# A decoder layer whose last, quantised FFN gets its weights and input ready-made, and runs its block and token loops as one

## The reference

```python
def act_quant(x):
    scale = 127.0 / jnp.clip(jnp.max(jnp.abs(x), axis=-1, keepdims=True), 1e-05)
    return jnp.clip(jnp.round(x * scale), -128, 127) / scale
def weight_quant(w):
    scale = 1.0 / jnp.clip(jnp.mean(jnp.abs(w)), 1e-05)
    return jnp.clip(jnp.round(w * scale), -1, 1) / scale
# x = x + FFN(layernorm(x)), with w1 (2048, 512) and w2 (512, 2048)
h = bit_linear(x, w1)                    # act_quant(x) @ weight_quant(w1).T
h = depthwise_conv1d(h, conv_w, conv_b)  # 3 taps along the tokens, zeros at both ends
h = jax.nn.silu(h)
return bit_linear(h, w2)
```

## Time and profile before

| | |
|---|---|
| median of 3 runs | 3668.49 us (3667.8 to 3669.5) |
| the profiled execution | 3668.09 us, of which the span from first to last instruction is 3666.5 us |
| PE busy | 3195.8 us (87%) |
| DVE busy | 2299.4 us (63%) |
| ACT busy | 1861.1 us (51%) |
| POOL busy | 1074.4 us (29%) |
| mean granted clock of TensorE | 0.945 of full speed |
| `cross_ffn` | some 2280 to 3043 us |
| `quantised_ffn` | 3043 us to the end |

### The profile page before, as it was taken

How to read it: one execution, slowest core, us unless ns; L and a number is a source line. 1 busy time by engine, 2 the same in 40 slices (tenths; PEclk the granted TensorE clock), 3 DMA queues, 4 the chain that set the end, 5 groups by cost and what they waited for, 6 DMA issues and landing times. The chain is left out here.

```text
span 3666.5 us, 56984 instructions
## 1 busy us (share of the span) xinstructions
PE 3195.8 (87%) x19244; PEld 2328.8 (64%) x19284; DVE 2299.4 (63%) x4086; ACT 1861.1 (51%) x3035; POOL 1074.4 (29%) x831
## 2 busy tenths in 40 slices
PE   6998999999999998699978995999999992576576
PEld 5776666666666665577756774788888881244244
DVE  6444888888888886455536886323232227878876
ACT  2123888888888887122223221422222223777676
POOL 2223131131132121423213553111111111466555
PEclk9999999999999999899988998999999995798898
DMA  4544122121122121655435442211111104021111
GB/s 153 183 161 132 56 89 63 54 89 60 57 88 61 57 80 56 230 206 197 168 121 166 138 138 98 98 35 35 35 34 34 35 24 150 6 70 33 37 46 41
DMA packets 224825, 331.24 MB, mean 90 GB/s; under 512 B 26768, under 2 KB 113840, under 8 KB 224176
## 3 DMA queue, kind: packets, MB, share of 16 engines
q1 hardware_dynamic: 199536, 293.54, 24.3%
q10 hardware_dynamic: 22016, 25.17, 1.9%
q0 software_dynamic: 3136, 10.80, 0.9%
HBM read 200.20 MB, written 129.24 MB: 90 GB/s over the span
## 5 line engine op out<-in xcount | busy, mean ns | idle before, releaser
L704 DVE CUSTOM_DVE_ANT_0 attend_scores<-attend_scores,attend_bias_table 128x1024 f32<-128x1024 f32 x512 | 630.5, 1232 | 163.5 <-PE attend_scores L558 156.9
L631 ACT ACTIVATE attend_probs<-attend_scores,attend_neg_max 128x1024 f32<-128x1024 f32 x512 | 571.5, 1116 | 136.3 <-DVE attend_neg_max L704 127.0
L570 PE MATMUL attend_turned<-attend_ident,attend_probs 128*128 128x128 f32 x4096 | 557.3, 275 | 11.4 <-DVE attend_probsT L712 11.2
L570 PEld LDWEIGHTS attend_turned<-attend_ident,attend_probs 128*128 128x128 f32 x4096 | 472.6, 141 | 121.4 <-DVE attend_probsT L712 32.7
L558 PE MATMUL attend_scores<-attend_k_stack,attend_q_stack 96*128 96x512 f32 x1024 | 374.9, 448 | 14.4 <-DMA attend_q_stack<-qk_parts 9.4
L1937 DVE TENSOR_TENSOR cross_ffn_h_lo<-cross_ffn_hidden,cross_ffn_h_hi 128x512 fp32r<-128x512 f32 x128 | 91.5, 720 | 466.6 <-ACT cross_ffn_h_hi L1876 466.6
L639 ACT COPY attend_probsT<-attend_turned 128x512 f32<-128x512 f32 x640 | 359.5, 583 | 25.2 <-PE attend_turned L570 23.4
L1873 ACT ACTIVATE cross_ffn_hidden<-cross_ffn_h_acc,cross_ffn_b_cols 128x512 f32<-128x512 f32 x128 | 88.3, 690 | 484.5 <-PE cross_ffn_h_acc L1814 484.5
L585 PE MATMUL attend_out_acc<-attend_probsT,attend_v_in 128*32 128x256 f32 x4096 | 312.9, 389 | 0.7 <-DVE attend_out_full L722 0.7
L532 POOL TENSOR_TENSOR attend_out_parts<-attend_out_full,attend_out_parts 128x256 fp32r<-128x256 f32 x64 | 46.7, 729 | 855.8 <-ACT attend_out_parts L646 855.8
L712 DVE COPY attend_probsT<-attend_turned 128x512 f32<-128x512 f32 x384 | 263.4, 686 | 1.0 <-PE attend_turned L570 1.0
(11 more groups left out here) (292 smaller groups left out, 6604.1 us busy)
## 6 DMA issues: line engine op xcount, KB each, us to landing
qk_parts<-qkv_qk_out SPq DMA_DIRECT2D x64, 512.0 KB, 3.1
attend_k_stack<-qk_parts SPq DMA_DIRECT2D x192, 128.0 KB, 2.5
attend_q_stack<-qk_parts SPq DMA_DIRECT2D x192, 128.0 KB, 2.6
o_parts<-attend_out_parts ACTq DMA_DIRECT2D x64, 256.0 KB, 2.5
mix_in_o_in<-o_parts SPq DMA_DIRECT2D x32, 512.0 KB, 6.5
qkv_x_in<-x SPq DMA_DIRECT2D x8, 1024.0 KB, 5.7
v_rows<-qkv_v_out SPq DMA_DIRECT2D x32, 256.0 KB, 2.3
attend_v_in<-v_rows SPq DMA_DIRECT2D x128, 64.0 KB, 1.8
```

The costliest lines, as they stand in the source:

```text
L570: last = pe.transpose(turned[:, x, c], probs[:, i % 2, k * P:(k + 1) * P], ident[:, :])
L631: act.activation(probs[:, i % 2], scores[:, i % 2], ACT.Exp, bias=neg_max[:, i % 4:i % 4 + 1], scale=-1.0, accum_out=den[:, qg % 2, j, h:h ...
L704: dve.tensor_tensor_reduce(scores[:, i % 2], scores[:, i % 2], bias_table[:, h, at:at + T], -1.0, BIG, ALU.add, ALU.min, neg_max[:, i % 4: ...
```

## The change

Three stages are edited.

`project_qkv` also prepares the last FFN's weights. In its first batch POOL loads w1 and w2 in eight pieces of 1 MB, ACT sums their absolute values; PE adds up, DVE makes `w_mean` (`mean_weights`). In the four halves of batches 1 and 2 they are loaded again, one group of each a half, scaled (ACT), clipped and rounded (DVE, `round_group`), turned (PE, `turn_group`, at blocks 8 and 10), copied (ACT) and stored in bf16 to `w1T_parts` and `w2T_parts`. The opening is reordered: x's second half is loaded after all weights, weight chunks 1 and 3 are split on POOL, and the second half is turned inside the first products. The loop over batches is written out.

`cross_ffn` also makes the last FFN's input. Inside half n, DVE makes statistics of half n-1 of x2 (`x_factors`, at block 4) and normalises, scales and rounds it (`quantise_x`, blocks 6 to 9); PE turns it (`turn_x`, blocks 8 to 11), ACT copies, SP stores `xq_parts` and the token scales `x_units`. The ring of `h_hi` and `h_lo` goes from 4 to 2.

`quantised_ffn` loads what these made and has one loop for everything:

```diff
-            pe.wait_ge(wT_ready, GROUPS)
-            sequences(pe, body)
+        def slots(work, turn):
+            for u in range(UNITS + 1):
+                for f in range(HB):
+                    if u < UNITS:
+                        work(u, f)
+                    turn(u, f)
+            for f in range(8):
+                turn(UNITS + 1, f)
+        def tile_at(u, f, back):
+            j = (u - 1) * HT + f // 4 - back
+            return j if 0 <= j < TILES else None
 # SP, ahead of its slots
-                for k in range(4):
-                    sp.dma_start(w1_raw[:, k * 4:(k + 1) * 4], w1[k * D:(k + 1) * D, :].rearrange("(c p) n -> p c n", p=P))\
-                        .then_inc(w_loaded[k], 16)
...
+                load_x(0)
+                sp.dma_start(w1T[:, :, :], w1T_parts.rearrange("k p n -> p k n")).then_inc(w_loaded[0], 16)
+                load_x(1)
+                sp.dma_start(w2T[:, :, :], w2T_parts.rearrange("f p n -> p f n")).then_inc(w_loaded[1], 16)
 # POOL
+                def work(u, f):
+                    i = u * HB + f
+                    pool.wait_ge(right_ready, i + 1)
+                    pool.wait_ge(left_added, i + 1)
+                    pool.tensor_tensor(conv[:, i % CR], conv[:, i % CR], right_tap[:, i % 2], ALU.add).then_inc(right_added, 1)
+                def turn(u, f):
+                    j = tile_at(u, f, 1)
+                    if j is not None and f % 4 in (0, 1):
+                        round_h(j, range(2 * (f % 4), 2 * (f % 4) + 2))
 # PE
+                def edge_products(b):
+                    pe.wait_ge(xq_loaded[b % 2], (b // 2 + 1) * 16)
+                    past(pe, y_ready, 2 * b * HB - 1)
+                    for f in range(HB):
+                        for k, col in ((0, P - 1), (1, 0)):
+                            for c in range(KB):
+                                last = pe.matmul(acc[:, 0, 2 * f + k:2 * f + k + 1], w1T[:, c, f * P:(f + 1) * P],
+                                                 xqT[:, b % 2, HT - 1 + k, c * P + col:c * P + col + 1], start=c == 0, stop=c == KB - 1)
+                    last.then_inc(edges_ready, 1)
+                def work(u, f):
+                    if f == 0 and s == 0:
+                        pe.wait_ge(edges_done, b + 1)
+                    past(pe, y_ready, i - 1)
+                    for c in range(KB):
+                        last = pe.matmul(acc[:, i % 2], w1T[:, c, f * P:(f + 1) * P], xqT[:, b % 2, s * HT:(s + 1) * HT, c * P:(c + 1) * P],
+                                         start=c == 0, stop=c == KB - 1)
+                    last.then_inc(h_ready, 1)
+                def turn_hq(j, groups):
+                    past(pe, hqT_ready, j * 2 + groups[0] // 2)
+                    for g in groups:
+                        pe.wait_ge(hq_ready, j * 4 + g + 1)
+                        for k in range(4):
+                            at = (g * 4 + k) * P
+                            last = pe.transpose(turned[:, (g % 2 * 4 + k) * P:(g % 2 * 4 + k + 1) * P], hq[:, j % 2, at:at + P], ident16[:, :])
+                    last.then_inc(hq_turned, 1)
+                def turn(u, f):
+                    r = f % 4
+                    here, last, before = (tile_at(u, f, back) for back in range(3))
+                    if r == 0 and before is not None:
+                        w2_product(before, range(HB // 2, HB))
+                    if r in (1, 2):
+                        groups = range(2 * (r - 1), 2 * r)
+                        if here is not None:
+                            turn_h(here, groups)
+                        if last is not None:
+                            turn_hq(last, groups)
+                    if r == 3 and last is not None:
+                        w2_product(last, range(HB // 2))
+                    if f == HB - 1 and u % 2 == 1 and u < UNITS - 1:
+                        edge_products(u // 2 + 1)
 # DVE (a slot's work, then its share of the tiles)
+                def work(u, f):
+                    i = u * HB + f
+                    dequantise(i)
+                    if i:
+                        add_left(i - 1)
+                    if by_dve(i):
+                        centre(i)
+                def turn(u, f):
...
+                    r = f % 4
+                    if r == 1 and before is not None:
+                        finish(before)
+                    if r == 2 and here is not None:
+                        find_max(here, range(0, 2))
+                    if r == 3 and here is not None:
+                        find_max(here, range(2, 4))
+                        scale_h(here)
+                    if f == HB - 1 and u % 2 == 1 and u < UNITS - 1:
+                        find_edges(u // 2 + 1)
 # ACT
+                    if r == 0 and last is not None:
+                        round_h_up(last)
+                    if r in (1, 2) and last is not None:
+                        copy_hq(last, range(2 * (r - 1), 2 * r))
```

More of the change, by code:

```diff
@@ L230, in pair @@
                                 .then_inc(qk_lo_ready, 1)
-                with pool.Fori(0, B - 1) as b:
-                    pair(b, False)
-                pair(B - 1, True)
+                            if weights == "sum" and f % 2 == 0:
+                                load_for_sum(4 * h + f // 2)
+                            if weights == "round" and f == 0:
+                                load_group(n)
+                        if weights == "round":
+                            store_group(n)
+                pair(0, "sum")
+                pool.wait_ge(wq_summed, 8)
+                for b in range(1, B - 1):
+                    pair(b, "round")
+                pair(B - 1, None)
+                for m in range(2):
+                    pool.wait_ge(wq_stored[m], 4 * 16)
             @block.tensor
@@ L267, in products, with pair @@
                         last.then_inc(acc_ready, 1)
[L269 removed]
+                def pair(b, last, weights):
                     for h in range(2):
[L271 removed]
+                        if not (last and h == 1) and not (isinstance(b, int) and b == 0 and h == 0):
                             turn(b * 2 + h + 1, (h + 1) % 2)
[L273 removed]
+                        products(b * 2 + h, h, weights)
                 turn(0, 0)
[L276 to L278 removed]
+                pair(0, False, False)
+                pe.wait_ge(wq_const, 3)
+                add_up()
+                for b in range(1, B - 1):
+                    pair(b, False, True)
+                pair(B - 1, True, False)
             @block.scalar
@@ L1935, in step @@
                         i = n * HB + j
+                        if not (isinstance(n, int) and n == 0):
+                            if j == FACTORS_AT:
+                                x_factors(n - 1)
+                            if FIRST_X <= j < FIRST_X + HT:
+                                quantise_x(n - 1, j - FIRST_X)
                         dve.wait_ge(hhi_ready, i + 1)
@@ new lines, in w2_product @@
+                def w2_product(j, blocks):
+                    if blocks[0] == 0:
+                        past(pe, out_done, j)
+                    for f in blocks:
+                        if f % 8 == 0:
+                            pe.wait_ge(hqT_ready, j * 2 + f // 8 + 1)
+                        last = pe.matmul(out_acc[:, :], hqT[:, j % 2, f * P:(f + 1) * P], w2T[:, f], start=f == 0, stop=f == HB - 1)
+                    if blocks[-1] == HB - 1:
+                        last.then_inc(out_ready, 1)
```

884 lines of the change are left out of this document (431 added, 453 removed).

## The result

The changed kernel takes **3776.6 us** (median of 4 runs, 3773.6 to 3777.4) against 3668.8 for the kernel before on the same chip (4 runs, 3667.8 to 3669.5): ratio 1.029, 95% interval 1.028 to 1.031. It is 108 us slower; 3743 was forecast, from 3630 to 3840. Its profiled span is 3775.7 us, against 3666.5.

A forecast was written before the change was run, and what follows sets the result against it. In the last stage's alternating block and token phases no engine is full in both; joined, in-order waits bound it. Profiled run 3668.1 - 63 (opening) + 108 (loop) + 30 (FFN before) + 0 (first stage) = 3743 us, range 3630 to 3840.

The forecast's parts named there:

- the first stage: Stage with `project_qkv`: earlier start minus 11, paid back by transposes and collisions; 0 in sum (ends minus 10, plus 15).
- the joined loop: Last stage, blocks and token tiles in one loop: 641 us against 533.1, plus 108 (ends minus 68, plus 190).
- the FFN before: `cross_ffn`, gaining a second normalisation and rounding: plus 30 us (ends 20 and 50), 18 of it after its last matmul.
- the opening: Start of the last stage, now only loads and edge products: 27 us against 90.4, minus 63 (ends minus 68, minus 50).
- The ring: Joined loop: next block's product waits until the present one has gone round three engines, twice a tile; 18.2 us at full clock.
- Rival A: Joined loop: waits overlap and the engines' work sets the pace, 12.9 us a tile, kernel 3567 us; chance 0.18.
- its point of decision: Rival A holds as soon as GpSimd's roundings don't stand behind a block that TensorE still has to feed.
- Rival C: Joined loop: only one of two rounds exposed, 15 to 17 us a tile, kernel 3620 to 3685; chance 0.15.
- the three borders: Joined loop, between batches: 128 edge products delay TensorE's next block, 9.3 us each at mixed clock, 28 for three.
- a share of 0.28 at the lower level: Joined loop: TensorE's time at 1.2 GHz, from the old block phases' mean 0.86; lifts a tile from 18.2 to 19.4.
- The scalar engine's 11.4 us a tile: Joined loop: the scalar engine's summed busy work per four slots (3x0.71 + 4x0.61 + 4x0.57 + 2.8 + 1.9).
- Rival B: Joined loop: TensorE stays at the lower clock throughout, 22.4 us a tile, kernel 3836 us; chance 0.12.

The follow-up runs named there:

- the best version: Version with TensorE a block ahead, GpSimd's roundings first, sums spread, w2T and scales store earlier; plus every second block's centre tap on VectorE: 3550.5 us, 0.968.
- Fillers: Changed kernel plus four products of 512 columns, result overwritten, in front of each of TensorE's two groups of transposes of the rounded tile: 3745.2 us, 1.020.

## Why the prediction was right, and where not

Measured against forecast, on the spans: 3775.7 against 3741.5, 34 too little: 17.3 of it in the first stage, 8.9 in the joined loop, 7.4 in the FFN before and 1.4 in stages with no edit, less 0.7 in the opening.

- **The ring** was the right mechanism. Its signs are there: roundings followed by the transposes after 0.14 and 0.06 us, TensorE idle on GpSimd (132.8 us in 32 tiles, 4.2 a tile where I had said some 6), VectorE and the scalar engine at 51 and 58%, a tile just over 20 us. Rival A is excluded for this order of instructions, and its point of decision was right: with GpSimd's roundings out of the ring a tile takes 14.3, and 12.3 in the best version, where A had 12.9. Rival C, one of two rounds exposed, is refuted by the timeline (from VectorE's read of one product to that of the next 7.37 and 7.16 us in the two rounds, both exposed).
- **The joined loop**: 641 forecast, 650 measured. VectorE's reads of the 1st, 17th, 21st and 128th product give the parts:

```profile
3127.76 0.69 DVE L2536 TENSOR_TENSOR quantised_ffn_y<-quantised_ffn_acc,quantised_ffn_unit_row 128x512 f32<-128x512 f32 x1 [9.15 <-PE quantised_ffn_acc L2409]
...
3160.16 0.68 DVE L2536 TENSOR_TENSOR quantised_ffn_y<-quantised_ffn_acc,quantised_ffn_unit_row 128x512 f32<-128x512 f32 x1
...
3171.43 0.68 DVE L2536 TENSOR_TENSOR quantised_ffn_y<-quantised_ffn_acc,quantised_ffn_unit_row 128x512 f32<-128x512 f32 x1
...
3729.45 0.69 DVE L2536 TENSOR_TENSOR quantised_ffn_y<-quantised_ffn_acc,quantised_ffn_unit_row 128x512 f32<-128x512 f32 x1 [4.55 <-PE quantised_ffn_acc L2409]
```

  The first product adds 2. The 16 slots without a tile took 32.4 (33 forecast), the next four 11.3 (10), the tail 46.3 (46). The 107 slots between took 558: 540 for 26.75 tiles, 20.2 each (19.4 for 27, 524), and 18 for the three borders (28). So it is in part luck that the loop came out only 9 off: the tiles were 16 more and the borders 10 less. The term that was mis-sized is the tile, and in it the clock: I took a share of 0.28 at the lower level from the old block phases; the mean of 0.79 is a share of 0.42, and 18.2 + 0.42 x 4.2 = 20.0. On the timeline the products of both rounds run at the lower level (1.91 us for four) and those of slots 3 and 0 at the higher one (1.03); by the prediction's own price of 1.0 a round that is 18.2 + 2.0 = 20.2. The borders were less since the 128 edge products take 3.55 us, 0.028 each, half of my lower bound: I had only the price of a 128-column transpose for a product of one column. The scalar engine's 11.4 us a tile is wrong twice, which touched rival A's 12.9 alone, as it was not on the path: the terms give 11.6, and by the prices above them they should have been 0.81, 0.71 and 0.61 for 0.71, 0.61 and 0.57, with which the sum is 12.4.
- **The opening**: 26.7 against 27, 63.7 less than before. The end of the load of w2T sets it, as forecast. It was issued late, as SP stood for 8.78 us in the load ahead of it; with w2T moved ahead of the second batch's input the opening took 22.

```profile
3089.00 0.43 SPq L1963 DMA_DIRECT2D x_units<-cross_ffn_x_unit  x1
3099.09 0.39 SPq L2316 DMA_DIRECT2D quantised_ffn_xqT<-xq_parts  x1
...
3102.02 8.78 SPq L2319 DMA_DIRECT2D quantised_ffn_unit_row<-x_units  x1
3110.85 0.48 SPq L2343 DMA_DIRECT2D quantised_ffn_w2T<-w2T_parts  x1
...
3114.57 3.55 PE L2399 MATMUL quantised_ffn_acc<-quantised_ffn_xqT,quantised_ffn_w1T 128*128 128x1 bf16 x128 [26.59 <-DMA quantised_ffn_w1T<-w1T_parts]
```

- **The FFN before**: 37.4 against 30. Under the products it lost 13.8 (12 forecast: 5 for `h_lo`, 7 for `turn_x`). The tail took 41.2 from the last product to the next stage's first load, against 17.5, so 23.6 in place of 18. The bare part up to the last store's issue took 18.8 more, by the prediction's own terms 19.0 (5.9 + 11.6 + 1.5; it has 18 for them). The step that failed is "then the stores, whose landing a store had before too": the store of x, 1 MB, lands in 4.2 us, and the one of 512 single numbers that now comes last in 8.9. So 5.2 us lay between the last store's issue and the next stage's first load, and now it is 10.1.
- **The first stage**: 17.3 against 0, outside my bound of 15, and the term with the worst reasoning. The start was won (the first read of a product at 32.1, minus 6.9, where I had 28: VectorE normalises the second half first). The transposes cost 7.8 (7 forecast). What was missing is an order: I put the scalar engine's and the queue's work "under the products" by its sum, 8 us in a half of 36, and did not ask what stands behind the instruction that waits for each 1 MB load. It was `round_x`, the scalar engine's rounding of x for the next half. 10 us of it went with the sums spread out; some 6 more in the first half were not tried.
- Stages with no edit took 1.4 longer in all.
- **Rival B** would have given 3836: the clock follows the waits, slot by slot, and does not stay down.

## What to carry to other kernels

When two phases are joined into one loop to fill engines, write down for each engine what stands in front of the instruction that feeds the next round, not only the sum of its work: here TensorE was busy for 14.3 us of a tile at its mixed clock and no other engine for more than 10.9, and a tile took 20.2, since a transpose that waits for the last step of a tile stood ahead of the product that starts the next block. Issuing the feeding product one slot ahead of whatever waits (with the copies a slot later) added no work and gave 176 us (180). The same question belongs to work that is "hidden" in an earlier stage: a load that lands late costs what is queued behind its reader.

## What the runs showed of the hardware that I had not expected

- A VectorE instruction with a single input from SBUF is drawn out by GpSimd as well: the centre tap (`tensor_scalar`, f32) takes 0.54 us alone and 1.26 to 1.49 beside an add or a rounding. The Trainium skill (SBUF — State Buffer, "Who interferes with whom") says that `tensor_scalar` can run in a mode that takes both port pairs. The trace agrees: the centre tap took 0.80 for 1024 numbers and takes 0.54 for 512, so 512 more cost 0.26, while a maximum of 4 numbers takes 0.16 and one of 512 takes 0.68, so that 508 more cost 0.52: the centre tap runs at twice the rate of the maxima. The maxima, by the same page, have no such mode. Those of h stay at 0.68 in every run, but they read PSUM and so prove little; `x_max` of the kernel before, which reads SBUF, took 0.69 in all 32 cases, 24 of them beside a GpSimd instruction. And whichever of the two engines begins second is the one that waits, as the two cases above show.
- A product with one column takes 0.028 us in a row of 128 (3.55 us in the opening, at a granted clock of 0.50, and 3.38 at the borders between batches, at 0.94 to 0.96): it hardly depends on the clock.
- SP's queue holds its engine: behind 4.5 MB of loads the next one took 8.78 us to issue, where the same load took 0.57 with 1 MB ahead of it. With w2T moved up it was the load of xqT behind it (5.5 MB ahead) that took 12.36. So it is the place in the queue that costs, not the kind of load.
- A store of single numbers took long whatever their count: 8.0 to 8.9 us from issue to landing for 512 of them, 7.7 for 128, where a store of 128 KB took 1.7 alone and 6.7 behind such a store.
- Fillers raised the granted clock from 0.79 to 0.90, and moving the waits to between 0.89 and 0.95.
